# Attention's last batch: the rows of quads 0 and 1 are turned two steps later

## The reference

```python
def attention(x, w_att_val, wv_w, wv_b, out_w, out_b):    # 16 heads, D = 16
    x_h = x.reshape(b, t, h, d).transpose(0, 2, 1, 3)
    xw = einsum('bhtd,hde->bhte', x_h, w_att_val)
    att = softmax(einsum('bhte,bhse->bhts', xw, x_h) / sqrt(d))
    vx = x @ wv_w.T + wv_b                                # per head
    o = einsum('bhts,bhsd->bhtd', att, vx)
    return o.reshape(b, t, e) @ out_w.T + out_b

def ffn(x, w_gate, w_up, w_down):                         # every operand quantized to FP4 in blocks of 16
    h = silu(fp4_linear(x, w_gate)) * fp4_linear(x, w_up) # 704 wide
    return fp4_linear(h, w_down)

x = x + attention(layernorm(x), ...)
x = x + ffn(layernorm(x), ...)
```

## Time and profile before

| | |
|---|---|
| median of the runs | 1459.87 us |
| the profiled execution's own time | 1459.96 us |
| its span | 1458.0 us |
| busy, share of the span: TensorE, VectorE, ScalarE, GpSimd | 97%, 87%, 59%, 45% |
| mean granted TensorE clock | 0.989 |
| last batch of attention, from its first maxima to the first matmul of the feed-forward block | 868.13 to 920.87 us |

### The profile page before, as it was taken

How to read it: one execution, slowest core, us unless ns; L and a number is a source line. 1 busy time by engine, 2 the same in 40 slices (tenths; PEclk the granted TensorE clock), 3 DMA queues, 4 the chain that set the end, 5 groups by cost and what they waited for, 6 DMA issues and landing times. The chain is left out here.

```text
span 1458.0 us, 32405 instructions
## 1 busy us (share of the span) xinstructions
PE 1421.5 (97%) x8612; PEld 892.2 (61%) x8612; DVE 1264.2 (87%) x2652; ACT 866.0 (59%) x1731; POOL 659.2 (45%) x911
## 2 busy tenths in 40 slices
PE   6899999999999999999999998999999999999999
PEld 4445555555555555555555554577777777777776
DVE  6788888888888888888888887699999999999996
ACT  1577777777777777777777777443333333343333
POOL 3455545545545545546546522234343343434341
PEclk8799999999999999999999999999999999999999
DMA  6856456455456455465455451000000000000000
GB/s 204 235 147 186 123 146 189 123 149 184 122 155 180 123 156 176 127 157 173 131 157 154 133 155 46 1 18 15 14 18 14 18 14 18 14 17 15 14 19 22
DMA packets 99785, 148.09 MB, mean 102 GB/s; under 512 B 21024, under 2 KB 58272, under 8 KB 99744
## 3 DMA queue, kind: packets, MB, share of 16 engines
q1 hardware_dynamic: 82672, 137.22, 32.9%
q10 hardware_dynamic: 17072, 10.37, 2.7%
HBM read 85.02 MB, written 65.27 MB: 103 GB/s over the span
## 5 line engine op out<-in xcount | busy, mean ns | idle before, releaser
L1199 DVE TENSOR_REDUCE neg_max<-ring 128x1 f32<-128x512 f32 x1016 | 636.0, 681 | 82.0 <-PE ring L929 81.7
L1081 ACT ACTIVATE probs<-scores 128x512 f32<-128x512 f32 x1024 | 534.3, 604 | 171.0 <-PE scores L940 165.7
L1714 PE MATMUL gu_bank<-splits,f_x_T 128*128 128x352 f32 x1024 | 313.7, 459 | 0.1
L929 PE MATMUL ring<-x_stack,q_stack 64*128 64x512 f32 x1016 | 230.7, 450 | 20.5 <-DVE neg_max L1199 11.4
L1714 PEld LDWEIGHTS gu_bank<-splits,f_x_T 128*128 128x128 f32 x1024 | 189.6, 190 | 95.4 <-ACT f_x_T L1688 0.5
L962 PE MATMUL ring<-probs,v_quad 128*32 128x512 f32 x2048 | 246.4, 599 | 0.2
L937 PE MATMUL scores<-q_stack,x_stack 64*128 64x512 f32 x1024 | 206.7, 397 | 2.7 <-DMA max_stack<-max_rows 1.5
L940 PE MATMUL scores<-max_stack,max_ones 64*128 64x512 f32 x1024 | 204.2, 392 | 0.0
L929 PEld LDWEIGHTS ring<-x_stack,q_stack 64*128 64x128 f32 x1016 | 98.0, 187 | 172.7 <-DVE neg_max L1199 114.5
L1404 POOL TENSOR_TENSOR f_small<-f_small,eps 128x1 f32<-128x1 f32 x64 | 42.9, 671 | 296.0 <-DVE f_small L1371 296.0
L1673 ACT ACTIVATE h_T<-h_bank 128x256 f32<-128x256 f32 (+1 forms) x128 | 56.0, 488 | 169.9 <-PE h_bank L1728 169.9
(11 more groups left out here) (144 smaller groups left out, 2015.5 us busy)
## 6 DMA issues: line engine op xcount, KB each, us to landing
x_rows<-splits SPq DMA_DIRECT2D x128, 256.0 KB, 3.8
x_stack<-x_rows SPq DMA_DIRECT2D x126, 256.0 KB, 4.0
q_stack<-q_rows SPq DMA_DIRECT2D x248, 128.0 KB, 4.0
q_rows<-splits SPq DMA_DIRECT2D x64, 256.0 KB, 2.2
out_dram<-x_all SPq DMA_DIRECT2D x64, 128.0 KB, 1.7
x_all<-in_L_attn_x_dram ACTq DMA_DIRECT2D x14, 512.0 KB, 4.2
w_raw<-slabs SPq DMA_DIRECT2D x14, 192.0 KB, 3.9
slabs_kept<-w_turned SPq DMA_DIRECT2D x14, 192.0 KB, 5.3
```

The lines of the kernel that those rows point to most:

```text
L929: pe.matmul(max_bank(b, g, ROWS * n + m)[:, :], row_tile(q_stack[q], m)[:, p, s * P:(s + 1) * P], row_tile(x_stack[q], m)[:, p, :], start= ...
L1081: act.activation(probs[j][:, k, :], scores[k][:, :], ACT.Exp).then_inc(p_ready, 1)
L1199: dve.tensor_reduce(neg_max[q % 2][:, at:at + 1], max_bank(b, g, k)[:, :], AX.X, ALU.max, negate=True).then_inc(m_used, 1)
L1714: m = pe.matmul(gu_bank[c][:, :], x_T[u][:, a, :], gate_up_T[:, a, c * CH:(c + 1) * CH], start=(a == 0), stop=(a == HALVES - 1))
```

## The change

Two new kinds of tile, `LATE_ROWS`, stand for rows 0 and rows 1 in the last batch alone. There the transposes, the reciprocal and the multiply of quad 0 move from step (1,1) to step (1,3), and those of quad 1 from step (2,1) to step (2,3), ahead of "proj0". In the list of the ring each is followed by three empty places (`None`), so that all other tiles keep their banks. The other fifteen batches are as before.

```diff
+    LATE_ROWS = ("rows0 of the last batch", "rows1 of the last batch")
+
...
     IN_STEP = {(0, 1): ("x0", "rows2", "turn0"), (0, 3): ("q0", "x1", "rows3"), (1, 1): ("weights", "turn1", "rows0"),
-               (1, 3): ("v0",), (2, 1): ("q1", "rows1"), (2, 3): ("proj0",), (3, 1): ("v1",), (3, 3): ("proj1", LAST_ROWS)}
+               (1, 3): ("v0", LATE_ROWS[0]), (2, 1): ("q1", "rows1"), (2, 3): (LATE_ROWS[1], "proj0"), (3, 1): ("v1",), (3, 3): ("proj1", LAST_ROWS)}
...
             if j % 2 == 0:
                 TILES_IN_RING.append(("pv", g, j // 2))
             else:
-                TILES_IN_RING += IN_STEP[g, j]
+                for kind in IN_STEP[g, j]:
+                    TILES_IN_RING += [kind] + [None] * (len(ring) - 1 if kind in LATE_ROWS else 0)
...
-        if kind == LAST_ROWS:
+        if kind == LAST_ROWS or kind in LATE_ROWS:
             return isinstance(b, int) and b == B - 1
+        if kind in ("rows0", "rows1") and isinstance(b, int) and b == B - 1:
+            return False
...
-        usual = [k for k in kinds if k != LAST_ROWS]
+        usual = [k for k in kinds if k != LAST_ROWS and k not in LATE_ROWS]
```

## The result

| | before | with the change |
|---|---|---|
| median of the runs | 1460.38 us (1459.0 to 1463.24, 22 runs) | 1463.42 us (1461.08 to 1466.74, 22 runs) |
| ratio after/before | | 1.0019, 95% interval 1.0014 to 1.0025 |
| the profiled execution: time, span, granted clock | 1459.96 us, 1458.0 us, 0.989 | 1465.82 us, 1463.8 us, 0.988 |

The further runs of the kernel before put its median half a microsecond above that of the first three. The change costs by the ratio 0.0019 x 1460.4 = 2.8 us, between 2.0 and 3.7 by its interval. That is slower, and less than 0.3%.

A forecast was written before the change was run, and what follows sets the result against it. The prediction took TensorE, busy nearly all the time, to bound the kernel. Its terms, 1.28 - 0.51 + 1.46 = +2.23 us, on the profiled execution's 1459.96 us gave 1462.2 us, range 1460.3 to 1464.2.

The forecast's parts named there:

- Step (1,1): Last batch, quad 0's transposes leave: they filled a wait that is there anyway, so TensorE gains 0.
- Step (1,3): Last batch, quad 0's transposes arrive: the next maxima wait for VectorE's multiply behind four reductions, +1.28 us.
- Step (2,1): Last batch, quad 1's transposes leave: the GpSimd wait goes, but key scores wait for ScalarE's exponentials, -0.51 us.
- Step (2,3): Last batch, quad 1's transposes arrive: the projection waits for VectorE's multiply, +1.46 us, of which 0.90 is stall.
- Sum: Last batch, where TensorE reaches quad 3's first step: +2.23 us in all, and nothing behind takes it up.
- Waits hidden: At both new waits VectorE reads the banks out before TensorE asks: no change, 1460.0 us; chance 0.10.
- Stall recovered: Where quad 1's transposes leave, the whole 1.64 us comes back: faster, 1458.9 us; chance 0.04.
- Clock falls: TensorE's granted clock leaves 1.00 after 893 us in the last batch: clearly slower, about 1479 us; chance 0.03.

The follow-up runs named there:

- rows 0 alone: The changed kernel edited so only quad 0's rows are moved and quad 1's stay in their old place; 1462.72 us against 1460.94 before (ratio 1.0011).
- rows 1 alone: The changed kernel edited so only quad 1's rows are moved and quad 0's stay in their old place; 1462.07 us against 1460.94 before (ratio 1.0006).
- second profile: The changed kernel built, profiled and timed again, unedited; 1463.13 us against 1460.62 before (ratio 1.002).
- read sooner: The changed kernel with VectorE taking quad 0's reciprocal and multiply ahead of the last of four reductions; 1462.68 us against 1460.62 before (ratio 1.0021).
- rows 1 in (3,1): The changed kernel with quad 0's rows back in place, quad 1's two steps later in another bank; ratio to before 0.9983, again 0.9995.
- before, again: The kernel before with one name's text altered and the same instructions; 1459.82 us against 1460.62 (ratio 0.9996).

## Why the prediction was right

The forecast was 1462.2 us, no change by the 0.3% bound; 1463.42 lies 1.2 above it and inside the range. Step by step, against the distances:

- **Step (1,1), gain 0.** Held. The first maxima of (1,2) wait 0.54 us for the same reduction in place of the transposes, and start 1.20 us behind "turn1" in both kernels. VectorE did idle longer (0.97 us instead of 0.77 ahead of the eight reductions' place), as argued.
- **Step (1,3), +1.28.** Measured +1.24 in the change and with rows 0 alone. The mechanism is shown from two sides: another bank takes the wait away (5.92 instead of 7.15), and VectorE sent sooner shortens it (6.79).
- **Step (2,1), -0.51.** Measured -0.41, and -0.43 with rows 1 alone. The name of what is late next was right: both waits are for ScalarE, and the second pair of key scores starts 904.67 - 898.33 = 6.34 us behind step (2,0), where before it took 900.63 - 893.77 = 6.86: 0.52 sooner. But from there to the values it now takes 0.67 us (904.67 to 905.34), and before 0.56. The pair at 904.67 stands behind a wait of 0.25 and takes 0.34 us to the next group, at 905.01; before, the same pair followed the first one at once and took 0.23 (900.63 to 900.86). It isn't the wait alone: the first pair before, right behind the transposes and without a wait, took 0.33 as well (900.07 to 900.40). The prediction carried the start of the pair forward and took the rest as unchanged, which made this term 0.10 too large. It also named one wait for ScalarE, of about 0.6, where there are two, 0.71 and 0.25.
- **Step (2,3), +1.46.** Measured +1.46, of which 0.81 is named as wait and 0.65 is the transposes (0.90 and 0.56 were forecast). With another bank it is 0.49.
- **Sum, +2.23.** Measured +2.29, and +2.30 in the second profile. The terms missed by -0.04, +0.10 and 0, so the sum isn't right by luck. It is +2.8 by the ratio of the times, whose interval of 2.0 to 3.7 holds both. Nothing behind (3,0) took it up: 14.76 to 14.79 us to the feed-forward block in every profile.
- **Rivals.** Waits hidden: refuted, both waits are there. Its sum, +0.05, is near what a different choice of banks gives (+0.20). Stall recovered: refuted by its own point of decision; the second pair of (2,2) would have had to start 899.6 - 893.77 = 5.83 us behind (2,0), and started 6.34 behind it. Clock falls: the granted clock is 1.00 in the stretches of the change (above) and in those from 877 to 906.71 us of its second profile, through both new waits. The reason given, that TensorE stays busy for more than four fifths, is weaker than it reads: the last section shows the clock falling in this batch, behind other short waits.

Of the 1.2 us between the forecast and the median, 0.4 is the level: the sum was laid on a profiled execution of 1459.96 us, while the kernel before has its median at 1460.38. The other 0.8 is the difference of the medians, 3.04 us against the forecast 2.23. The distances give 2.29 and the second comparison 2.5, so most of this 0.8 looks like scatter of the start; no run shows that it is.

## What to carry to other kernels

In a ring of buffers, the cost of moving a tile can lie less in its own work than in who gets its buffer next: give the tile a buffer that the instructions right behind it don't need before judging the place. Here 2.09 of 2.29 us hung on the banks alone, through one wait for VectorE's queue of reductions and one for a full round trip to VectorE, and the same order with other banks cost 0.20. A wait that is removed ahead of a second wait gives back only the difference, and a move that lands in a wait and in a free buffer costs nothing (step (3,1)). Where the start of the program scatters by several microseconds, measure distances from the last point ahead of the change, and do not believe a ratio that promises six times what the trace contains.

## What the hardware showed beside

**Where the scatter comes from.** The same instructions bring step (1,2) of the last batch to anywhere between 886.18 and 892.14 us. Most of it arises near the start. The first projection of the program starts between 135.42 and 140.24 us over the ten profiles, 4.8 us apart, and the last one ahead of the last batch between 863.28 and 868.43, 5.2 apart, and no profile's lead over the kernel before changes by more than 0.4 us in between. The rest comes in between there and step (1,2). TensorE waits for loads near the start, and again in step (1,0) of the last batch. Two rows of the change's TensorE timeline:

```profile
76.96 0.50 PE L934 MATMUL ring<-x_stack,q_stack 64*128 64x512 f32 x2 [1.92 <-DMA q_stack<-q_rows]
...
884.62 0.51 PE L942 MATMUL scores<-q_stack,x_stack 64*128 64x512 f32 x2 [0.73 <-DMA max_stack<-max_rows]
```

The first of these waits was between 0 and 2.76 us over the ten profiles, but it doesn't set the start by itself: "read sooner" has the longest and reaches the first projection at 137.82, "rows 1 alone" has none there and reaches it at 138.93. The second was absent in three profiles and 0.22 to 0.92 in the others: quad 1's maxima come back from DRAM late there. Those of quads 2 and 3 were in time in every profile, as the prediction had it for step (3,0). The part that varies is the store. ScalarE issues it at 876.97 in the change and the load at 882.63, behind a wait of 2.17 for the store; over the ten profiles 4.58 to 5.84 us lie between the two, and the profiles without a wait of TensorE have 4.58, 4.95 and 5.04, those with 0.92 have 5.84 and 5.77. "Read sooner" doesn't fit (4.60, and a wait of 0.22). In the kernel before, three such pairs between 312 and 357 us lie only 3.2 to 3.7 us apart, where the DMA engines' share is 0.69 and 0.59 (340 to 350, 350 to 360); in the last batch it is 1.11 (870 to 880), since the weights of the feed-forward block are being fetched. That the fetch is what slows the store is read from this and not tested.

**A clock that falls for one step.** In two of the ten profiles (rows 1 alone, and the second of rows 1 in (3,1)) the granted clock dropped inside step (1,0), ahead of the waits that the change adds. TensorE's timeline of the second one:

```profile
882.06 0.66 PE L1001 MATMUL ring<-ident,pv_rows 128*128 128x128 f32 x4 [0.81 <-DVE neg_max L1206]
882.65 0.50 PE L936 MATMUL ring<-x_stack,q_stack 64*128 64x512 f32 x2
884.07 0.50 PE L944 MATMUL scores<-q_stack,x_stack 64*128 64x512 f32 x2 [0.92 <-DMA max_stack<-max_rows]
...
886.03 3.10 PE L969 MATMUL ring<-probs,v_quad 128*32 128x512 f32 x16
```

and its stretches from there, with the columns of the stretches above:

```profile
884.00:888.00 4.00, 3.93 (x22) 1.51 (x26) 1.95 (x4) 2.73 (x6) 0.42 (x2) 0.63 0.00 0
888.00:892.00 4.00, 3.78 (x28) 1.89 (x20) 2.40 (x4) 2.53 (x6) 1.29 (x2) 0.94 0.00 0
```

TensorE was busy for 3.93 of 4 us at a mean granted clock of 0.63, that is largely at 1.2 GHz, right behind two waits of 0.81 and 0.92, and was back near full in the next stretch. The sixteen matmuls on the values took 3.10 us instead of 1.92. From the transposes at 882.06 to the first maxima of step (1,2) it took 10.08 us, and in the second profile of the change, which had the same two waits there and a clock of 1.00 throughout, 8.55 (877.63 to 886.18): this fall cost 1.5 us. In "rows 1 alone" the clock fell behind waits of 0.81 and 0.32, and in "before, again" the same two left it at 1.00. So such waits don't decide it by themselves, and what else does, or whether they are the cause, no run here shows.

The Trainium skill (TensorE: Matmul & The Clock Gate, "A second HAM failure mode: psum-queue depth-cycling") says that frequent brief idle times between groups of matmuls can swing the clock between half and full. The prediction held against it that the trace does not agree. That is too strong: at the two new waits no profile shows a fall, but in quad 1 of the same batch two profiles do. It is a part of why a span can be late, and no part of the change's 2.29.
